# Expert blocks of a mixture-of-experts layer: the down product as three fp32r products in place of one fp32 product

## The reference

```python
def _L0_ffn_ref(x, Wg, W1, W2, W3):
    scores = jnp.einsum('btd,ed->bte', x, Wg)
    topk_s, topk_i = jax.lax.top_k(scores, TOP_K)          # TOP_K = 2, E = 8
    probs = jax.nn.softmax(topk_s, axis=-1)
    ...
    for e in range(E):                                     # D = 512, H = 352
        h = jax.nn.silu(jnp.einsum('btd,hd->bth', x, W1[e])) * jnp.einsum('btd,hd->bth', x, W2[e])
        y = y + w[..., e:e + 1] * jnp.einsum('bth,dh->btd', h, W3[e])
    return y
```

## Time and profile before

| | |
|---|---|
| median of 3 runs | 898.68 us (895.45 to 900.51) |
| profiled execution | 900.36 us, span 898.5 us |
| PE matmul / PE weight load busy | 738.7 us (82%) / 589.0 us (66%) |
| DVE / ACT / POOL busy | 522.3 us (58%) / 424.3 us (47%) / 250.9 us (28%) |
| expert blocks: down product L1134 | 120 records of 592 ns |
| expert blocks: weight remainders L1535 on DVE | 40 of 1623 ns |
| POOL in the expert blocks: gathers L688 | 20 of 1563 ns |

### The profile page before, as it was taken

How to read it: one execution, slowest core, us unless ns; L and a number is a source line. 1 busy time by engine, 2 the same in 40 slices (tenths; PEclk the granted TensorE clock), 3 DMA queues, 4 the chain that set the end, 5 groups by cost and what they waited for, 6 DMA issues and landing times.

```text
span 898.5 us, 13420 instructions
## 1 busy us (share of the span) xinstructions
PE 738.7 (82%) x4533; PEld 589.0 (66%) x4533; DVE 522.3 (58%) x1065; ACT 424.3 (47%) x790; POOL 250.9 (28%) x284
## 2 busy tenths in 40 slices
PE   0899998601899999966988989989987688999984
PEld 0698777501777777766977868778774355777752
DVE  4876675641566666346475474564664435777773
ACT  3423665332555555211376375574664413554552
POOL 1002344212121211044065083182351001222232
PEclk9895998755999999985899999999999998999997
DMA  8545144996375556775001001000013920210000
GB/s 265 198 148 169 54 137 137 334 374 248 85 243 171 175 177 173 257 210 146 1 12 47 26 27 38 33 23 33 25 38 146 356 112 35 74 56 10 10 18 19
DMA packets 51793, 108.71 MB, mean 121 GB/s; under 512 B 12149, under 2 KB 30321, under 8 KB 48953
## 3 DMA queue, kind: packets, MB, share of 16 engines
q1 hardware_dynamic: 48605, 99.50, 33.0%
q0 software_dynamic: 3136, 8.53, 3.6%
HBM read 88.59 MB, written 19.43 MB: 120 GB/s over the span
## 4 chain that ended last, share of the span: by engine, by line
PE 45%; issue 19%; DVE 11%; DMA 9%; POOL 7%; ACT 5%; SPq 2%; ACTq 1%; POOLq 0%; DVEq 0%
PE PS L148 10%; PE PS L150 9%; PE PS L149 9%; POOL wraw L736 4%; PE PS L1134 3%; PE PS L1479 3%; PE PS L1195 2%; DMA w_scratch<-wraw 2%; PE PS L1496 2%; ACT w_hi L788 2%; DMA raw<-wkv_in 1%; DMA fq_raw<-foldq_in 1%; PE PS L1238 1%; DMA fp_raw<-foldp_in 1%; DVE wscale L1734 1%
## 5 line engine op out<-in xcount | busy, mean ns | idle before, releaser
L736 POOL TENSOR_TENSOR wraw<-wraw,rinv 128x361 f32<-128x361 f32 (+1 forms) x104 | 80.9, 791 | 140.2 <-DVE rinv L1692 140.1
L1535 DVE TENSOR_TENSOR w_lo<-w,w_hi 128x1408 fp32r<-128x1408 f32 x40 | 64.9, 1623 | 35.3 <-ACT w_hi L788 34.5
L884 ACT ACTIVATE wraw<-PS,nmx 128x361 f32<-128x361 f32 (+1 forms) x104 | 58.7, 565 | 37.9 <-DVE nmx L1699 30.1
L1699 DVE TENSOR_REDUCE nmx<-PS 128x1 f32<-128x361 f32 (+1 forms) x104 | 55.1, 530 | 33.5 <-PE PS L150 33.1
L763 POOL TENSOR_TENSOR wraw<-gs,us 100x352 f32<-100x352 f32 x32 | 30.3, 947 | 153.9 <-ACT gs L1054 125.5
L148 PE MATMUL PS<-pf_hi,cx_hi 128*100 128x512 f32 x128 | 55.1, 431 | 8.9 <-DVE pf_lo L1870 3.7
L148 PE MATMUL PS<-w_hi,xt_hi 128*128 128x352 f32 x160 | 57.0, 356 | 6.5 <-DVE xt_lo L1529 6.5
L688 POOL DMA_INDIRECT xb<-xn_scratch,rows x20 | 31.3, 1563 | 109.7 <-PE PS L1108 107.3
L788 ACT CAST w_hi<-w 128x1408 fp32r x40 | 54.7, 1369 | 10.3 <-issue 10.3
L1702 DVE TENSOR_TENSOR pt_lo<-PS,pt_hi 128x384 fp32r<-128x384 f32 x96 | 52.3, 546 | 12.0 <-ACT pt_hi L890 11.1
L1294 PE MATMUL PS<-ident,wraw 128*128 128x128 f32 x312 | 52.0, 276 | 6.2 <-POOL wraw L736 3.4
(11 more groups left out here) (272 smaller groups left out, 2041.8 us busy)
## 6 DMA issues: line engine op xcount, KB each, us to landing
w<-w_in SPq DMA_DIRECT2D x20, 768.0 KB, 5.5
w<-w_in SPq DMA_DIRECT2D x8, 1408.0 KB, 12.1
fq_raw<-foldq_in SPq DMA_DIRECT2D x6, 1088.0 KB, 7.7
cx_raw<-ctx_scratch SPq DMA_DIRECT2D x8, 800.0 KB, 5.5
ctx_scratch<-ctxo SPq DMA_DIRECT2D x24, 256.0 KB, 2.0
ys_scratch<-yb SPq DMA_DIRECT2D x20, 256.0 KB, 5.7
wraw<-wup_in SPq DMA_DIRECT2D x12, 256.0 KB, 4.4
raw_even<-wupt_in SPq DMA_DIRECT2D x4, 768.0 KB, 5.1
```

The lines of the kernel that those rows point to most:

```text
L736: pool.tensor_tensor(P1[slot][0:rows, 0:NK], P1[slot][0:rows, 0:NK], rinv[0:rows, jj, t:t + 1].broadcast_to((rows, NK)), ALU.mult).then_in ...
L884: act.activation(P1[t % 8][r, 0:NK], PS[r, t % 4, 0:NK], ACT.Exp, bias=nmx[r, jj, t:t + 1], accum_out=rsum[r, jj, t:t + 1]).then_inc(C["ex ...
L1535: dve.tensor_tensor(WL[which][:, :], w12_of(dve_wlo.e, which), WH[which][:, :].bitcast(F32), ALU.subtract) \
L1699: dve.tensor_reduce(nmx[r, jj, t:t + 1], PS[r, t % 4, 0:NK], AX.X, ALU.max, negate=True).then_inc(C["max"], 1)
```

## The change

The down product is made as the gate and up products are, by `mm3`: nine fp32r matmuls instead of three fp32 matmuls. For that both of its inputs are split. DVE writes `HT` as fp32r and then the remainder `HTL` from the same bank (one buffer). ACT rounds the block's down weights into `W3H` (one buffer, 3 pieces of 512 columns), and POOL subtracts, in the same three pieces, into `W3L`, which lies in the place of the raw weights. PE waits for each piece ahead of its three matmuls. `route` and `xn` are allocated right below `wraw`, because `W3H` takes their place; ACT waits once for the end of the routing (`route`, 3) ahead of its first block.

```diff
-        HT = [at(f"ht{i}", [128, FHP], MOE_AT + 20 * D + 4 * FHP * (4 + i)) for i in range(2)]
+        HT = [at(f"ht{i}", [128, FHP], MOE_AT + 20 * D + 4 * FHP * (4 + i), F32R) for i in range(2)]
+        HTL = at("ht_lo", [128, FHP], MOE_AT + 4 * D, F32R)
+        W3H = at("w3_hi", [128, W3], -4 * (W12 + W3) - 4 * W3, F32R)
+        W3L = [at(f"w3_lo{i}", [128, W3], W3_AT + 4 * W3 * i, F32R) for i in range(2)]
...
-            for i in range(NBLK):
+            def gather(i):
                 wait(pool, E["xtp"], i - 1)
                 pool.indirect_dma_start(XB[i % 2][:, :], None, xn_scratch,
                                         bass.IndirectOffsetOnAxis(ap=rows[:, i:i + 1], axis=0)).then_inc(XS[i % 2], 16)
+            def pool_w3lo(i):
+                for c in range(len(FC)):
+                    w = slice(c * D, (c + 1) * D)
+                    pool.wait_ge(E["w3h"], len(FC) * i + c + 1)
+                    pool.tensor_tensor(W3L[i % 2][:, w], W3R[i % 2][:, w], W3H[:, w].bitcast(F32), ALU.subtract).then_inc(E["w3l"], 1)
+            gather(0)
+            gather(1)
+            for i in range(NBLK):
+                if i + 2 < NBLK:
+                    gather(i + 2)
+                pool_w3lo(i)
...
+            act.wait_ge(E["route"], 3)
...
+        def act_w3hi(act, i):
+            act.wait_ge(W3S[i % 2], 16 * (i // 2 + 1))
+            wait(act, E["yps"], i)
+            for c in range(len(FC)):
+                w = slice(c * D, (c + 1) * D)
+                act.copy(W3H[:, w], W3R[i % 2][:, w]).then_inc(E["w3h"], 1)
...
                 act_silu1(act, i)
                 if i + 1 < NBLK:
                     act_whi(act, i + 1, 0)
                     act_xt(act, i + 1)
                     act_whi(act, i + 1, 1)
+                act_w3hi(act, i)
                 if i > 0:
                     act_y(act, i - 1)
...
         def pe_y(pe, i):
-            pe.wait_ge(E["ht"], i + 1)
-            pe.wait_ge(W3S[i % 2], 16 * (i // 2 + 1))
+            pe.wait_ge(E["ht"], 2 * i + 2)
             wait(pe, E["yb"], i - 1)
             for c, rows in enumerate(FC):
-                last = pe.matmul(PS[:, 4 + i % 2, :], HT[i % 2][0:rows, c * 128:(c + 1) * 128],
-                                 W3R[i % 2][0:rows, c * D:(c + 1) * D], start=(c == 0), stop=(c == len(FC) - 1))
+                pe.wait_ge(E["w3l"], len(FC) * i + c + 1)
+                h, w = slice(c * 128, (c + 1) * 128), slice(c * D, (c + 1) * D)
+                last = mm3(pe, PS[:, 4 + i % 2, :], HT[i % 2][0:rows, h], HTL[0:rows, h], W3H[0:rows, w], W3L[i % 2][0:rows, w],
+                           c == 0, c == len(FC) - 1)
             last.then_inc(E["yps"], 1)
...
             dve.tensor_copy(HT[i % 2][:, :], PS[:, 3, 0:FHP]).then_inc(E["ht"], 1)
+            dve.wait_ge(E["ht"], 2 * i + 1)
+            wait(dve, E["yps"], i)
+            dve.tensor_tensor(HTL[:, :], PS[:, 3, 0:FHP], HT[i % 2][:, :].bitcast(F32), ALU.subtract).then_inc(E["ht"], 1)
```

More of the change, by code:

```diff
@@ L351, in build_kernel @@
         E = sems("e", "consts wghi_ex wglo_diff gate gating picked ranks route cast_pad xnst "
-                      "w12 xs0 xs1 w30 w31 xtp xth gps ups silu h htp ht yps yb ys0 ys1 x")
+                      "w12 xs0 xs1 w30 w31 xtp xth gps ups silu h htp ht w3h w3l yps yb ys0 ys1 x")
         WHS, WLS, XTLS, ATT0 = (A["mx_wgh"], A["exp_wuh"]), (A["sub_wgl"], A["ptsb_wul"]), A["pv_xtl"], HG * B
@@ L1123, in pe_htp @@
             wait(pe, E["h"], i + 1)
-            wait(pe, E["ht"], i)
+            wait(pe, E["ht"], 2 * i)
             for c in range(len(FC)):
```

5 lines of the change are left out of this document (3 added, 2 removed).

## The result

| | before | after |
|---|---|---|
| median of the runs | 896.53 us (20 runs, 889.75 to 903.80) | 902.42 us (20 runs, 898.15 to 919.17) |
| the profiled execution, and its span | 900.36, 898.5 us | 902.31, 900.5 us |
| silu to silu in the expert blocks | 7.49 us | 7.70 us |
| first gather of x to first gather of results | 172.2 us | 177.1 us |

The ratio is 1.008, with a 95% interval of 1.005 to 1.011: 7 us slower, between 4 and 10. The medians differ by 5.9 us. The spans differ by only 2.0 us, because in this execution the stages ahead of the blocks happened to take 3.7 us less (first gather at 208.18 us, before at 211.84). Those stages are unchanged; their end varies from 204.7 to 211.9 us over all the profiles here. So I read the expert blocks by themselves. The changed kernel's times spread wider than the old one's; where the text compares, it uses the ratio and not single times.

A forecast was written before the change was run, and what follows sets the result against it. PE looked like the bound, with a 7.07 us chain beside it; port waits make blocks 7.66 us against 7.49, +3.1 us over 18 steps, plus tail 0.8: +3.9, 902.6 us. Range 893 to 910 (the forecast case's own 899 to 907).

The forecast's parts named there:

- The chain beside PE: Expert blocks: silu, gate cast, gate remainder, x remainder, gate product take 7.07 us; PE savings win at most 0.42 us a block.
- PE, nine matmuls in 2.07 us: Down product: nine fp32r matmuls 0.23 us apart replace about 2.58 us, 0.51 us less.
- ACT's casts 1.6 us, hidden: ScalarE: three down-weight casts a block wait for the down product and fit in the 1.33 us idle before silu.
- The h remainder 0.55 us, hidden: VectorE: h's remainder takes 0.55 us within 1.27 us of idle time ahead of the gate weights' remainder.
- The down weights' DMA, cost nothing: Wait before ScalarE's casts: reached some 5 us earlier, but the load has some 7 us against a 5.5 us median landing.
- POOL and the shared port: Three 1.27 us subtractions a block and VectorE's two-SBUF-input remainders wait for each other's whole operation; gate remainder over 2 us.
- P = 7.07 + (8.25 - P): Block pace when the gate remainder waits for POOL's end at about +10.5 us after silu: 7.66 us.
- The lock: VectorE reading two SBUF inputs and GpSimd reading SBUF exclude each other on shared ports for a whole instruction.
- The tail +0.8 us: After the last silu: down product waits for casts, pieces and matmuls, 9.4 us where it was 8.6.
- the port costs nothing: Rival: subtractions don't hold up VectorE's remainders in the blocks; -6.8 to -3.5 us, 892 to 895.5 us; chance 0.2.
- POOL is the bound, slower: Rival: port operations run strictly in a row, 8.0 us a block; +9.8 us, about 908.5 us; chance 0.18.
- A wash: Rival: half the waits fall on VectorE's idle time, PE's saving pays the rest; 7.49 us a block, 899.5 us; chance 0.12.

The follow-up runs named there:

- e1_memset: Changed kernel with each GpSimd subtraction replaced by three memsets of about equal length that read nothing, PE using the high half instead: 896.69 us.
- e2_cols384: Changed kernel with each GpSimd subtraction cut to 384 of 512 columns, PE using the high half in place of the remainder: 900.67 us.
- e11_dve0_load: Changed kernel with a block's first subtraction on VectorE, two on GpSimd, routing wait moved ahead of the x cast, register loads moved ahead: 889.94 us, ratio 0.990.
- e9_before_load: Kernel before the change with register loads moved ahead, ScalarE's in front of silu and VectorE's in front of h's copy: 890.89 us, ratio 0.9936.
- e10_after_load: Changed kernel with the register loads moved ahead, ScalarE's before silu and VectorE's before h's copy, nothing else: 903.08 us, ratio 1.0066.
- e7_split_only: Changed kernel with all splitting kept but the down product in fp32 from raw weights; subtractions into one spare tile, each waiting for the last: 907.97 us.
- e6_six: Changed kernel with the down product leaving out h's remainder times the weights' high half, so six matmuls: 923.63 us.
- e4_dve0: Changed kernel with a block's first subtraction on VectorE, the other two on GpSimd, and the routing wait moved ahead of the x cast: 896.15 us, ratio 1.001.

## Why the prediction was right, and where not

The number was 902.6 us, measured 902.42; the range held. That is closer than the reasoning deserves, because two things met. I started from the median of three runs, 898.68 us, and over 20 runs it is 896.53. And I forecast +3.9 us where +5.9 (by the ratio +7) was measured. So the forecast difference was too small by 2 to 3 us, and on the side "slower by over 0.5%", to which I gave 0.39, not "within", to which I gave 0.45.

- **The chain beside PE, 7.07 us**: right. e1_memset and e2_cols384 settle at 7.16 and 7.15 us once the port wait is gone; e11_dve0_load, without the 0.17 us of issue, at 6.97. The longer step of the kernel before is the register loads', as read: e9_before_load. But that time taken off PE can win up to 0.42 us a block no longer holds once the loop is longer than the chain: there it wins nothing.
- **PE, nine matmuls in 2.07 us**: right.

```profile
372.00 0.39 PE L148 MATMUL PS<-w_hi,ht 128*128 128x512 f32 x1
...
373.86 0.39 PE L150 MATMUL PS<-w_hi,ht_lo 96*128 96x512 f32 x1
```

  Eight steps in 1.86 us, 0.23 each.
- **ACT's casts 1.6 us, hidden**: 1.66 us, and ACT is still idle for 0.73 us ahead of silu. Right: POOL asks for its first piece behind them, but while the up remainder still runs.
- **The h remainder 0.55 us, hidden**: 0.56 us, with 0.8 us of idle time behind it. Right.
- **The down weights' DMA, cost nothing**: right; the casts wait for PE alone.
- **POOL and the shared port**: right in kind and in size at this point. The pieces take 1.27 to 1.31 us, the first up to 2.58 when an up remainder is ahead of it. The gate remainder takes 2.0 to 2.25 us in most blocks (1.7 in three), and the forecast was "over 2 us". Pace 7.70 us for 7.66. The register load under the wait costs nothing: e10_after_load.
- **P = 7.07 + (8.25 - P)**: the number is right here, the dependence is wrong, and that is luck. The formula holds POOL's end at +10.5 us after silu. In the trace the up remainder stands in DVE's queue behind the gate remainder, and POOL behind the up remainder, so a late gate remainder delays POOL's end by as much: a loop of 7.69 us, in which silu doesn't stand. With the change's prices the two ways give nearly the same. They part when a price changes: 0.1 us more on a piece, which I put at 0.15 us on P, is 0.3 us by the loop. GpSimd's part longer by 0.36 us made the steady pace longer by 0.36, not 0.18 (e7_split_only); shorter by 0.84, it went down to the chain and not by half (e2_cols384).
- **The lock**: the Trainium skill, page "SBUF — State Buffer", section "SBUF: two separate sides", describes the lock as held for a whole instruction, and for a VectorE instruction with two SBUF inputs only against a GpSimd instruction that reads SBUF. The change agrees with the first (three pieces end 3.64 us behind the up remainder), e1_memset, the only run with GpSimd as busy and no read, with the second. My sum didn't have that one engine can keep the port over several instructions while the other waits. In e6_six and e10_after_load three subtractions in a row did so, in the change they didn't.
- **The tail +0.8 us**: last silu to last result copy is 9.87 us (forecast 9.4, before 8.65), +1.2, but the path from that copy to the first gather of the results was 1.4 us shorter than before, so in the end it cost nothing here (-0.2).
- **The step that failed: the start.** I priced the added wait for the routing at nothing. It keeps the table load from its idle place, 1.28 us on the path to the first silu. Pace 19 x 0.205 = 3.9, start 1.26, end -0.2: **4.9 us**, as first gather to first gather (177.1 against 172.2), inside the ratio's 4 to 10. So three errors partly cancel: pace 0.8 and start 1.3 us too low, tail 1.0 too high.

Of the rivals, "the port costs nothing" fell by the remainders. "POOL is the bound, slower" in its own form, the gather not through before the next first piece, didn't come true but was near: POOL's gather ends at 313.65 in the block shown and its next subtraction begins at 313.95, ended by the cast. "A wash" had the pace at 7.49 us, which no step shows. What set the pace is next to the first half of that rival, a loop of operations one behind the other over both engines; it was in the forecast's steps, but as a wait and not as a loop.

## What to carry to other kernels

When GpSimd gets an operation that reads SBUF, don't ask only whether GpSimd has room, but whose two-operand read on VectorE stands behind it; a run in which GpSimd is as busy but reads nothing tells the two apart. Before moving work off an engine that looks full, find the chain beside it: here register loads ahead of a cast and a remainder were worth more (5.7 us) than the 0.5 us a block taken off TensorE. Where a wait recurs in every block, follow it round until it meets itself: if the sum of the pieces is the pace, only what lies in that loop changes it. And when an experiment needs a wait that the kernel doesn't have, look for its price in the trace before reading the difference. A wait put between two instructions of ScalarE also moves a table load that was hidden between them.

## What the runs showed of the hardware that I had not expected

- One engine can keep the port over a row of operations, but needn't. DVE's 1.62 us remainder took 5.13 to 5.16 us in all seven cases of e6_six and e10_after_load in which it came 0.09 to 0.11 us behind the first of GpSimd's three subtractions. In the change it took 2.68 us when it came 0.10 us behind (and 2.40 when 0.36 behind). So the distance doesn't decide it.
- In e4_dve0 the two take turns in all blocks but the last: up remainder, GpSimd's first piece, DVE's own piece (1.77 us instead of 0.69), GpSimd's second (1.75 instead of 1.27).
- Handing over by a semaphore and not by the port costs 0.2 us a block (7.90 against 7.70 us). GpSimd's subtractions stand 0.14 us apart when each waits for the one before by a semaphore, and overlap by 0.04 us when it doesn't (e7_split_only).
- The same subtraction of 128x512 takes 0.63 us in a row on DVE and 1.27 us on GpSimd.
- ScalarE's register load varies between 0.27 and 1.06 us in one execution of the kernel before, and the variation is gone from the pace once the load stands where its engine idles anyway; there it took 0.27 to 0.49 us.
- Two of three stretched remainders in e10_after_load were followed by 3.4 us at a granted clock of 0.5, after which a block was 1.6 us longer than the third such block at 1.00.
